# Cross attention: normalise the probabilities on GpSimd before they are turned, instead of scaling the output

## The reference

```python
# second sublayer: x is the normed input, init the context; C = 64, T = 512, DQK = 64
q = jnp.einsum('dc,bct->btd', Wq, init) + bq
k = jnp.einsum('dc,bct->bdt', Wk, init) + bk[None, :, None]
R = jnp.einsum('btd,bds->bts', q, k)
attention = jax.nn.softmax(R, axis=-1)
v = jnp.einsum('oc,bct->bto', Wv, x) + bv
out = jnp.einsum('bts,bsc->bct', attention, v)
...
x = x + _L0_xattn_ref(_layernorm(x, axis=-1), ctx_4096, ...)
x = x + _L0_ffn_ref(_layernorm(x, axis=-1), L0_ffn_identity)
```

## Time and profile before

| | us |
|---|---|
| median of 3 runs (2224.16 to 2227.65) | 2226.3 |
| profiled execution | 2226.27 |
| its span | 2224.5 |
| PE busy | 2174.7 |
| DVE busy | 1415.3 |
| ACT busy | 1060.0 |
| POOL busy | 651.9 |

### The profile page before, as it was taken

The page is one execution under the profiler, slowest core; times in us unless marked ns, Lnnn a source line. Parts: engine busy times, 40 slices in busy tenths (PEclk is TensorE's granted clock), DMA queues, the critical chain, the costliest instruction groups (busy, mean ns, idle before and its releaser), DMA issues. The chain is left out here.

```text
span 2224.5 us, 37071 instructions
## 1 busy us (share of the span) xinstructions
PE 2174.7 (98%) x13600; PEld 1793.2 (81%) x13600; DVE 1415.3 (64%) x1925; ACT 1060.0 (48%) x1799; POOL 651.9 (29%) x723
## 2 busy tenths in 40 slices
PE   6999999999999999999999999999999999799998
PEld 6888888888888888878888888888888888455555
DVE  6666666666666666676666666666666665577775
ACT  4444444444444444444444444444444443566664
POOL 5333333333333332343322333333333331111110
PEclk9999999999999999999999999999999999899999
DMA  3111111111111111111111111111111110200000
GB/s 128 57 49 41 47 40 48 48 48 48 48 48 48 48 40 47 50 39 41 48 48 48 48 48 48 48 40 46 41 48 48 48 49 23 110 29 29 29 24 20
DMA packets 37915, 104.91 MB, mean 47 GB/s; under 512 B 4448, under 2 KB 9056, under 8 KB 37728
## 3 DMA queue, kind: packets, MB, share of 16 engines
q1 hardware_dynamic: 37856, 104.10, 14.4%
HBM read 99.89 MB, written 4.19 MB: 47 GB/s over the span
## 5 line engine op out<-in xcount | busy, mean ns | idle before, releaser
L733 PE MATMUL bank<-x_hi,w_hi 128*128 128x512 f32 x1344 | 531.4, 395 | 2.4 <-ACT gate L384 2.4
L736 PE MATMUL bank<-x_hi,w_lo 128*128 128x512 f32 x1344 | 524.2, 390 | 1.2 <-issue 1.2
L735 PE MATMUL bank<-x_lo,w_hi 128*128 128x512 f32 x1344 | 523.1, 389 | 0.0
L733 PEld LDWEIGHTS bank<-x_hi,w_hi 128*128 128x128 f32 x1344 | 252.2, 188 | 59.3 <-ACT gate L384 3.3
L736 PEld LDWEIGHTS bank<-x_hi,w_lo 128*128 128x128 f32 x1344 | 252.3, 188 | 54.1
L735 PEld LDWEIGHTS bank<-x_lo,w_hi 128*128 128x128 f32 x1344 | 252.5, 188 | 50.8
L748 PE MATMUL bank<-wv_hi,x_hi 128*128 128x256 f32 x1024 | 293.1, 286 | 0.0
L306 POOL TENSOR_TENSOR sq_acc<-sq_acc,sq 128x512 f32<-128x512 f32 x124 | 160.5, 1295 | 445.7 <-ACT sq L434 432.5
L749 PE MATMUL bank<-wv_lo,x_hi 128*128 128x256 f32 x1024 | 290.4, 284 | 0.0
L750 PE MATMUL bank<-wv_hi,x_lo 128*128 128x256 f32 x1024 | 290.3, 283 | 0.0
L295 POOL TENSOR_TENSOR qk<-qk,sq 128x512 f32<-128x512 f32 x64 | 83.0, 1296 | 701.0 <-ACT sq L397 701.0
(11 more groups left out here) (124 smaller groups left out, 3442.9 us busy)
## 6 DMA issues: line engine op xcount, KB each, us to landing
raw<-w_pairs SPq DMA_DIRECT2D x96, 512.0 KB, 3.4
raw<-w_v SPq DMA_DIRECT2D x32, 512.0 KB, 3.4
raw<-w_out SPq DMA_DIRECT2D x32, 512.0 KB, 3.3
ctx<-ctx_in SPq DMA_DIRECT2D x16, 256.0 KB, 2.8
xr<-x SPq DMA_DIRECT2D x4, 1024.0 KB, 10.9
out<-attn_acc SPq DMA_DIRECT2D x16, 256.0 KB, 2.0
attn_acc<-x SPq DMA_DIRECT2D x8, 256.0 KB, 6.5
decays<-decay SPq DMA_DIRECT2D x32, 64.0 KB, 1.9
```

The lines of the kernel that those rows point to most:

```text
L733: nc.tensor.matmul(bank[:, to], w_hi[:, a, s], x_hi[:, b, c], start=part in ("first", "only") and c == 0, stop=False, skip_group_check=True)
L735: nc.tensor.matmul(bank[:, to], w_hi[:, a, s], x_lo[:, b, c], start=False, stop=False, skip_group_check=True)
L736: i = nc.tensor.matmul(bank[:, to], w_lo[:, a, s], x_hi[:, b, c], start=False, stop=part in ("last", "only") and c == 1, skip_group_check= ...
```

## The change

The probabilities are multiplied by the inverse of their row's sum, in `prob` itself, by eight GpSimd instructions of 128 x 512 for each pair, before TensorE turns them. The reciprocals are taken in four pieces, one for each j. S and ScalarE's copy of it go, and `add_cross` is one instruction instead of two. Q moves ahead of T0 and writes bank `OUT` instead of `MISC`; so it waits for `x2_ready`, `add_cross` of the pair before. T0 waits for all eight normalised blocks instead of the eight `exps`.

```diff
+                def normalise(t, j):
+                    pool.wait_ge(S["inv_ready"], t * CH + (j + 1))
+                    for i in range(2):
+                        nc.gpsimd.tensor_scalar(prob[:, t % 2, i, j], prob[:, t % 2, i, j], row_inv[:, t % 2, j, i:i + 1],
+                                                None, ALU.mult).then_inc(S["normed_ready"], 1)
                 inv_root(2, 0, 0)
                 inv_root(2, 0, 1)
+                for j in range(CH):
+                    normalise(0, j)
                 for t in range(PAIRS):
                     if t:
                         inv_root(3, 1, t - 1)
+                    if t + 1 < PAIRS:
+                        normalise(t + 1, 0)
+                        normalise(t + 1, 1)
                     if t + 2 < PAIRS:
                         inv_root(2, 0, t + 2)
+                    if t + 1 < PAIRS:
+                        normalise(t + 1, 2)
+                        normalise(t + 1, 3)
...
 # ScalarE
+                    if t + 2 < PAIRS:
+                        keep_q(t + 2, OUT)
                     keep_turned(t, 0)
-                    if t + 2 < PAIRS:
-                        keep_q(t + 2, MISC)
...
-                    keep_scale(t)
...
 # VectorE
-                def inverse(t):
-                    dve.wait_ge(S["exp_ready"], 2 * CH * (t + 1))
-                    nc.vector.reciprocal(row_inv[:, t % 2], row_sum[:, t % 2]).then_inc(S["inv_ready"], 1)
+                def inverse(t, j):
+                    dve.wait_ge(S["exp_ready"], 2 * (t * CH + j + 1))
+                    nc.vector.reciprocal(row_inv[:, t % 2, j], row_sum[:, t % 2, j]).then_inc(S["inv_ready"], 1)
...
-                    dve.wait_ge(S["scale_ready"], t + 1)
-                    nc.vector.tensor_tensor(scale[:, :], bank[:, OUT], scale[:, :], ALU.mult)\
-                        .then_inc(S["scaled"], 1)
-                    dve.wait_ge(S["scaled"], t + 1)
-                    nc.vector.scalar_tensor_tensor(out=x1[:, t], in0=scale[:, :], scalar=pre.bias[:, 2:3],
+                    nc.vector.scalar_tensor_tensor(out=x1[:, t], in0=bank[:, OUT], scalar=pre.bias[:, 2:3],
...
+                    if t + 1 < PAIRS:
+                        inverse(t + 1, 0)
                     keep_turned(t, 2)
                     if t + 1 < PAIRS:
+                        inverse(t + 1, 1)
                         keep_values(t + 1)
                         row_max(t + 1, 2, 0)
...
                         row_max(t + 1, 3, 2)
+                        inverse(t + 1, 2)
+                        inverse(t + 1, 3)
                     if t:
                         dve.wait_ge(S["xn3_ready"], t)
                     add_cross(t)
                     layernorm(3, 1, t)
-                    if t + 1 < PAIRS:
-                        inverse(t + 1)
...
 # TensorE
+                    if t + 2 < PAIRS:
+                        if t:
+                            pe.wait_ge(S["x2_ready"], t)
+                        project_q(t + 2, OUT)
                     turn(t, 0)
-                    if t + 2 < PAIRS:
-                        if t >= 2:
-                            pe.wait_ge(S["out_ready"], t - 1)
-                        project_q(t + 2, MISC)
                     turn(t, 1)
...
-                    spread_scale(t)
                     weigh(t, 0)
                     weigh(t, 1)
```

## The result

| | before | changed |
|---|---|---|
| median, us | 2225.23 (4 runs) | 2339.62 (4 runs, 2334.65 to 2340.58) |
| profiled execution, its span | 2226.27, 2224.5 | 2339.66, 2337.8 |

The changed kernel is slower by 5.1%: the ratio is 1.051, with a 95% interval of 1.049 to 1.053. I had forecast 2230.3.

The account below looks back on a forecast made before the run. TensorE was taken as the bound, its queue full and GpSimd nearly idle. Start +2.2, pair 0 to 1 +0.8, twelve pairs +2.8, pairs 14 and 15 +0.0, end -1.7: +4.1 on 2226.27, forecast 2230.3 us; 8-in-10 range 2225 to 2252.

Parts of the forecast that it names:

- Step 1: Between T0 and T1 on TensorE: without Q, T1 still waits for T0's copies, leaving a 0.87 us gap.
- Step 2: On TensorE, from weigh 0 onwards: without S, everything behind it starts 1.02 us earlier in each pair.
- the end: Last pair's path: S's 1.02 us and the multiplication's 0.68 + 0.03 go, -1.7 us.
- Steps 3 to 5: VectorE's queue: four reciprocals, last exps, then later add_cross, which Q awaits; T0 at 2068.82 instead of 2068.58.
- the start: Start of the stage: GpSimd's first eight blocks delay T1, +2.2 us (bounds +0.5 and +7); pair 0 to 1 adds +0.8.
- the pairs: Mid-stage: T0 comes +0.24 us later a pair, +2.8 us for the 12 pairs from pair 1 to pair 13.
- Step 6: GpSimd's two last blocks before T0: 0.70 us a block, bounds 0.61 and 1.30, hidden by Q up to 0.81.
- GpSimd becomes the bound: Rival, GpSimd's eight blocks before T0: at 1.30 us a block, +36 us, 2262; 10%.
- The rival of the shared ports in every pair: GpSimd's blocks 3 beside add_cross: the two engines hinder each other, T0 0.53 us later in twelve pairs, 2238; 8%.
- S comes back in full: Rival, TensorE: the full 1.02 us is saved in 16 pairs, -16.4 us, 2209.9; 5%.

Follow-up runs that it names:

- e1: The kernel before with only Q moved ahead of T0, into bank OUT: 2232.45 us, ratio 1.0035.
- e2: The kernel before without S, ScalarE's copy of it and the multiplication in add_cross, so the output stays undivided: 2208.73 us, ratio 0.9928.
- e3: The changed kernel with GpSimd's eight multiplications replaced by copies of the same block onto itself: 2230.2 us, ratio 1.0019.
- e4: The changed kernel with GpSimd's multiplication over only 256 of the 512 columns of each block: 2241.44 us, ratio 1.0078.
- e5: The changed kernel with each GpSimd block as a two-input multiplication, row_inv broadcast along the columns: 2247.65 us, ratio 1.0106.
- e8: The changed kernel with 32 unread transposes of the identity on TensorE ahead of T0's wait: 2298.07 us, ratio 1.0332.
- e10: The kernel of e9 with T0's transposes ordered by block and a separate wait for each block: 2216.44 us, ratio 0.9963.
- e11: The changed kernel with the constant 0.5 in place of the scalar per partition in GpSimd's multiplication: 2322.03 us, ratio 1.044.
- e9: The changed kernel with the eight multiplications on VectorE, add_cross behind them, Q back between T0 and T1 in bank OUT: 2219.24 us, ratio 0.9977.

## Why the prediction was wrong, step by step

- *Step 1, Q leaves the gap.* Right: 0.88 us before T1 in the kernels that have Q ahead of T0. Alone it cost 0.71 us a pair (e1), not 0.87.
- *Step 2, S goes.* Nearly right: 0.89 us a pair (e2) of the 1.02, and 1.7 at the end was 2.3 in e3.
- *Steps 3 to 5, the reciprocals, the last exps, add_cross ahead of Q.* Right in sum: with GpSimd at 0.62 us a block a pair took 18.74, where they give 18.93 (e3), and the whole kernel 2230.2 against the forecast's 2230.3. That this is so close is luck in part. Terms were off in opposite directions: the start, 7.1 up to T0 of pair 2 instead of 3.2, the pairs, +0.06 instead of +0.24, and the end.
- *Step 6, the price of a block, is the step that failed.* I wrote 0.70 us and gave 1.30 as the upper end; it is 1.57. The working took the copy's price for each column as that of any one-input instruction, and the two-input addition as a ceiling. Neither holds: a scalar multiplication costs 0.00249 us a column (e4) where I had estimated 0.00088 from the copy, and the two-input multiplication with a repeated value 1.05 us a block (e5). The ceiling wasn't one: in these runs the price goes by the form of the instruction and not by its number of inputs. The trace of before had one hint, which I passed over, the same form on one column and on eight (groups of the kernel before, columns as in the earlier trace rows):

```profile
L976 POOL TENSOR_SCALAR rstd<-mv 128x1 f32<-128x1 f32 x32 | 7.4, 232 | 273.2 <-DVE mv L1100 273.2
...
L254 POOL TENSOR_SCALAR rstd<-mv 128x8 f32<-128x8 f32 x1 | 0.3, 252 | 6.5 <-DVE mv L600 6.5
```

  Twenty ns for seven columns is 0.0029 us a column, 1.7 us for 512. The hint is a weak one: over the traces of this case the single column's mean runs from 218 to 244 ns against some 250 for eight columns, which gives anything from 0.8 to 2.7 us for 512, and in the trace of before four instructions of the same line on two columns took 581 ns on average. It was a reason to doubt the ceiling of 1.30, no more.
- *The rival "GpSimd becomes the bound" was what happened,* at a price above the one that I gave it. By its own reckoning, eight blocks from 2059.2 on with inv_root among them, 1.57 us (1.55 from start to start) gives 2072.8 and a T0 4.4 us late. e8, where the clock stays full, shows nearly this: 22.99 - 18.68 = 4.3 us a pair.
- *What no part of the prediction had is the clock in mid-stage.* I put half clock in at the start of the stage only. With a wait of 3.9 us ahead of T0, a pair takes 2.6 us more than with the wait filled (25.58 against 22.99). Of the 82.8 us over twelve pairs, 52 are GpSimd's chain and 31 the clock.
- *The rival of the shared ports in every pair* didn't happen: the blocks beside add_cross took the same as the others (in e5 four of the two-input form in 4.03 us, beside add_cross and away from it; in e3 two copies in 1.18 us beside it and in 1.17 away from it).
- *S comes back in full* didn't happen in any run. The most was 0.89 us of 1.02 without any normalisation (e2) and 0.77 with it (e10), both with Q in the gap.

## What to carry to other kernels

Price an instruction by the same form on the same engine, at any size that the trace has, before reaching for another form of the same shape. Two sizes that lie far apart give its slope (256 and 512 columns here); one and eight columns only showed that the ceiling was in doubt. Where the trace has no such row, no neighbour's price is a bound. When work moves to an idle engine, don't ask whether its busy time fits into the period, but how long its stretch is behind the last thing that it waits for: GpSimd was busy 28 of 50 us and set every pair. And where a wait opens in front of TensorE, add to its length what the clock takes from the instructions behind it, and prefer to put what work there is into the gap.

## What the runs showed of the hardware that I had not expected

- GpSimd, float32, 128 x 512, in place: copy 0.62 us (e3), multiplication by a tensor that repeats one column 1.05 (e5), by a constant 1.49 (e11), by a scalar for each partition 1.57 (the changed kernel); addition of two tensors 1.30. The GPSIMD Engine Reference of the Trainium skill (section 4.1) says that elementwise work with one input runs at roughly line rate; nothing here speaks against that for the copy, but the scalar form, at 2.5 times the copy's time, doesn't agree. Nor is it the best loop that the same page of the Trainium skill gives (section 3.1), 769 ns for 512 elements. VectorE does the same multiplication in 0.48 us (e9).
- A TensorE that has waited 3.9 us in a pair of 25.6 falls to 1.2 GHz, but not at a fixed place. In pair 7 T0 behind the wait still took 1.09 us and T1, K and the first scores ran at half speed; in pair 6 the clock had fallen within the wait (0.86 on average over 2078.0 to 2081.6) and T0 took 1.97. By weigh (1.94 us for what took 1.94 in e8) it had recovered in both. One pair of such a trace is therefore not the rule for the others. Keeping TensorE at work with products that nobody uses made the kernel about 40 us faster. The page TensorE: Matmul & The Clock Gate of the Trainium skill (section Part 1: The HAM clock gate) describes the level as following recent activity; the trace agrees, granted clock 0.86 with the waits and 1.00 with them filled.
- VectorE and GpSimd slowed each other where VectorE had two inputs in SBUF, both ways. In the changed kernel's start the four subtractions of eye_hi took 0.92 us each and not 0.69, and the eight blocks beside them 13.05 us and not 12.4, twice the 6.20 of four elsewhere. Beside the two-input form (e5) the subtractions took 1.51 us each, and the eight blocks 9.81 us and not 8.06, twice the 4.03 of four. The subtractions in the changed kernel:

```profile
L1145 DVE TENSOR_TENSOR eye_lo<-eye,eye_hi 128x512 fp32r<-128x512 f32 x4 | 3.4, 917 | 2.6 <-ACT eye_hi L1051 2.6
```
